# The last additions of a routed FFN, shared between VectorE and GpSimd

## What is computed

```python
def _L3_ffn_ref(x, gate_w, gate_b, w1, b1, w2, b2):
    flat = x.reshape(-1, D)
    logits = flat @ gate_w + gate_b
    topv, topi = lax.top_k(logits, TOP_K)                 # TOP_K = 2 of E = 8
    topw = jax.nn.softmax(topv.astype(jnp.float32), axis=-1)
    routing = jnp.zeros_like(logits).at[jnp.arange(T)[:, None], topi].set(topw)
    def body(acc, params):
        W1e, b1e, W2e, b2e, we = params
        h = jax.nn.gelu(flat @ W1e + b1e, approximate=False)
        return (acc + (h @ W2e + b2e) * we[:, None], None)
    final, _ = lax.scan(body, init, (w1, b1, w2, b2, routing.T))
...
x = x + jnp.tanh(g_ffn[3]) * _L3_ffn_ref(_layernorm(x, axis=-1), ...)
```

## Time and profile before

| | us |
|---|---|
| median of 3 runs | 1948.7 |
| the three runs | 1950.23, 1944.82, 1948.7 |
| span of the profiled execution | 1942.7 |
| busy in it: TensorE / VectorE / ScalarE / GpSimd | 1620.1 / 1242.5 / 1210.7 / 740.3 |

### The profile page before, as it was taken

How to read it: one execution, slowest core, us unless ns; L and a number is a source line. 1 busy time by engine, 2 the same in 40 slices (tenths; PEclk the granted TensorE clock), 3 DMA queues, 4 the chain that set the end, 5 groups by cost and what they waited for, 6 DMA issues and landing times. The chain is left out here.

```text
span 1942.7 us, 38924 instructions
## 1 busy us (share of the span) xinstructions
PE 1620.1 (83%) x12739; PEld 1206.0 (62%) x12739; DVE 1242.5 (64%) x3348; ACT 1210.7 (62%) x4192; POOL 740.3 (38%) x712
## 2 busy tenths in 40 slices
PE   4399999599999769999789966999579887866994
PEld 3355554379999546666589855545456555644994
DVE  5599999488888666767567755213457656654444
ACT  2189999189999557877667742433168656631444
POOL 2145555245555542111067835002222332333542
PEclk9799999699999889999889987999689888977997
DMA  3320000110000042423191022100044433313224
GB/s 127 74 106 1 1 1 1 34 45 2 1 2 2 28 116 76 105 72 89 32 320 54 1 88 86 42 0 1 19 121 114 124 101 84 88 55 97 70 70 156
DMA packets 63845, 126.40 MB, mean 65 GB/s; under 512 B 10670, under 2 KB 27233, under 8 KB 61529
## 3 DMA queue, kind: packets, MB, share of 16 engines
q1 hardware_dynamic: 53658, 103.10, 18.6%
q10 hardware_dynamic: 5616, 12.06, 1.9%
q0 software_dynamic: 4384, 8.89, 1.3%
HBM read 91.00 MB, written 50.43 MB: 73 GB/s over the span
## 5 line engine op out<-in xcount | busy, mean ns | idle before, releaser
L1531 ACT ACTIVATE L_E<-L_sc,L_negm 128x128 f32<-128x128 f32 x1024 | 300.1, 402 | 153.2 <-DVE L_negm L1399 152.5
L593 ACT ACTIVATE B_E<-B_logits,B_m 128x32 f32<-128x32 f32 (+1 forms) x1792 | 365.2, 374 | 8.8 <-DVE B_m L562 7.9
L599 POOL TENSOR_TENSOR B_E<-B_E,B_r 128x512 f32<-128x512 f32 x256 | 268.0, 1047 | 264.5 <-DVE B_r L581 264.5
L1399 DVE TENSOR_REDUCE L_negm<-L_sc 128x4 f32<-128x512 f32 x256 | 174.9, 686 | 87.0 <-PE L_sc L1640 74.9
L562 DVE TENSOR_REDUCE B_m<-B_logits 128x16 f32<-128x512 f32 (+1 forms) x256 | 172.8, 675 | 38.4 <-PE B_logits L553 31.2
L1638 PE MATMUL L_sc<-KS,L_QS 128*128 128x512 f32 x256 | 143.8, 562 | 54.5 <-DMA L_QS<-L_qsplit 37.1
L576 DVE TENSOR_REDUCE B_r<-B_E 128x16 f32<-128x512 f32 (+1 forms) x256 | 172.9, 675 | 2.5 <-POOL B_E L599 1.3
L1539 ACT ACTIVATE L_PT<-L_pt 128x512 f32<-128x512 f32 x256 | 165.9, 649 | 6.3 <-DMA picked_rows<-A_ys 6.0
L1648 PE MATMUL L_pt<-ident,L_E 128*128 128x128 f32 x1024 | 160.1, 280 | 0.8 <-ACT L_PT L1539 0.8
L551 PE MATMUL B_logits<-B_phihi,B_xhi 128*128 128x512 f32 x256 | 153.5, 600 | 5.1 <-DVE B_philo L538 2.5
L1648 PEld LDWEIGHTS L_pt<-ident,L_E 128*128 128x128 f32 x1024 | 126.6, 145 | 23.9 <-issue 2.5
(11 more groups left out here) (348 smaller groups left out, 3598.5 us busy)
## 6 DMA issues: line engine op xcount, KB each, us to landing
route_rows<-in_F_fill SPq DMA_DIRECT2D x33, 516.0 KB, 19.7
KS<-L_ksplit SPq DMA_DIRECT2D x180, 64.0 KB
L_QS<-L_qsplit SPq DMA_DIRECT2D x42, 256.0 KB
F_xg<-route_rows SPq DMA_DIRECT2D x71, 64.5 KB
ew<-in_expert_w SPq DMA_DIRECT2D x1, 4096.0 KB, 15.4
L_cT<-in_ctxT SPq DMA_DIRECT2D x16, 256.0 KB
L_qsplit<-L_qhi ACTq DMA_DIRECT2D x16, 256.0 KB, 2.7
L_qsplit<-L_qlo ACTq DMA_DIRECT2D x16, 256.0 KB, 5.8
```

The costliest lines, as they stand in the source:

```text
L593: ins = nc.scalar.activation(e[:, cols], self.bank(k)[:, cols], ACT.Exp, bias=self.m[:, k % 4, g:g + 1])
L599: self.st.nc.gpsimd.tensor_tensor(e, e, self.r[:, k % 2, :].unsqueeze(2) .to_broadcast([128, self.ng, self.size]), ALU.mult).then_inc(self ...
L1399: nc.vector.tensor_reduce(negm[:, k % 4, :], sc[k % 2][:].rearrange("p (h k) -> p h k", h=NHG), AX.X, ALU.max, negate=True).then_inc(s["ma ...
L1531: ins = nc.scalar.activation(e[:, h * 128:(h + 1) * 128], sc[k % 2][:, h * 128:(h + 1) * 128], ACT.Exp, bias=negm[:, k % 4, h:h + 1])
```

## The change

The adds of groups 1, 3, 5 and 7 go to GpSimd, behind its last scatter; VectorE keeps those of groups 0, 2, 4 and 6. The semaphore `x_new` becomes two, `x_new0` counted by VectorE and `x_new1` by GpSimd, and SP waits on them in turn.

```diff
@@ semaphores
-            "y_ps", "y_out", "init_ps", "init_used", "part_sum", "scaled", "x_new", "stored")}
+            "y_ps", "y_out", "init_ps", "init_used", "part_sum", "scaled", "x_new0", "x_new1", "stored")}
@@ sync
             for n in range(NG):
-                sp.wait_ge(s["x_new"], n + 1)
+                sp.wait_ge(s[f"x_new{n % 2}"], n // 2 + 1)
                 sp.dma_start(out[:, n * GB:(n + 1) * GB, :], xgroup(p, n)).then_inc(s["stored"], 16)
@@ gpsimd
             for i in range(NT):
                 bring(i)
+            for n in range(1, NG, 2):
+                g.wait_ge(s["part_sum"], n + 1)
+                g.wait_ge(s["scaled"], n + 1)
+                cols = slice(n * GB, (n + 1) * GB)
+                nc.gpsimd.tensor_tensor(xgroup(p, n), yl[0][:, cols, :], yl[1][:, cols, :], ALU.add).then_inc(s["x_new1"], 1)
@@ vector, total(n)
-                nc.vector.tensor_tensor(xgroup(p, n), yl[0][:, cols, :], yl[1][:, cols, :], ALU.add).then_inc(s["x_new"], 1)
+                nc.vector.tensor_tensor(xgroup(p, n), yl[0][:, cols, :], yl[1][:, cols, :], ALU.add).then_inc(s["x_new0"], 1)
@@ vector
                 ins.then_inc(s["part_sum"], 1)
-                if n:
+                if n % 2:
                     total(n - 1)
-            total(NG - 1)
```

## The result

| | before | with the change |
|---|---|---|
| median, 20 runs each (us) | 1944.73 | 1950.84 |
| lowest to highest | 1936.09 to 1951.29 | 1941.11 to 1960.34 |
| span of the profiled execution | 1942.7 | 1952.9 |

The ratio is 1.0034, with a 95% interval of 1.0020 to 1.0047: some 6 us slower, 4 to 9 by the interval. The forecast was +2.0. The time lies in the range, the sign was right, and two thirds of the loss were not foreseen. That the median of 1950.84 stands beside a forecast of 1950.7 is luck: the forecast added +2.0 to the median of three runs, 1948.7, and the median of twenty is 1944.73. The base was 4.0 us too high and the change priced 4.1 too low.

A forecast was written before the change was run, and what follows sets the result against it. VectorE was taken to bound the tail, with only its last 1 to 2 us to be bought. 3.24 + 1.13 - 2.40 = +1.97 us, on the median 1948.7, gave 1950.7 us; range 1945.5 to 1954.3.

The forecast's parts named there:

- four adds off VectorE: VectorE's tail loses four adds of 0.60 us each: 2.40 us off its chain.
- three adds of GpSimd in its stream: GpSimd's adds of groups 1, 3, 5 take turns with VectorE, costing it 1.08 us each: +3.24 us.
- the fourth, behind VectorE's last: GpSimd's add of group 7 ends 1.13 us after VectorE's last add: +1.13 us.
- last add: End of the tail's last add, on GpSimd: moves from 1938.99 to 1940.96, +1.97 us.
- last store, issue to landing: SP's store of group 7, issued in an idle queue, lands 2.1 us after issue, as before.
- closing: From the last store's landing to the kernel's end: 1.6 us, as before.
- The estimate from the Trainium skill: Exclusive turns held for whole instructions, 115 ns on each side: 4 x (1.27 + 2 x 0.115) - 2.40 = +3.6 us.
- The forecast signs: GpSimd adds 1.27 to 1.6 us, neighbouring VectorE instructions beyond 1 us, VectorE tail 13.0, last add's end at 14.2.
- Side by side: Rival 1: VectorE and GpSimd do not collide in the tail, -1.2 us, 1947.5; chance 0.15.
- Starvation of GpSimd: Rival 2: GpSimd's four adds come only when VectorE is through, +3.0 us, 1951.7; chance 0.22.
- rival 3: Each VectorE tail instruction loses its overlap and pays a gap as the port changes hands, +9.4 us, 1958.1; chance 0.04.
- rival 4: GpSimd's adds fall in VectorE's pauses, or the measured difference is that between runs: 1948.7; chance 0.09.

The follow-up runs named there:

- e4: Changed kernel without GpSimd's four adds, odd groups stored without their sum; no timed ratio, the end comes 14.7 us after group 1's first VectorE instruction.
- e1: Changed kernel with one more GpSimd DRAIN directly behind its last scatter, ahead of its four adds; timed 1.0017 (0.9993 to 1.0040).
- e3: Changed kernel, GpSimd drained behind its last scatter, VectorE's tail reading PSUM in place of a second SBUF tensor; no timed ratio, last add ends at 11.0 us.
- e6: Changed kernel, GpSimd drained behind its last scatter, X copied to eight PSUM banks by VectorE during its wait; timed 0.9987 (0.9969 to 1.0005) against before.
- e2: Kernel before, all adds on VectorE, plus a 128x4 GpSimd memset waiting for the last add; timed 1.0021 (0.9996 to 1.0046).
- e2b: Kernel before with the late GpSimd memset and a DRAIN directly behind the last scatter; no timed ratio, tail 16.0 us.
- e5: Changed kernel with one more GpSimd DRAIN ahead of the last eight scatters; single time 1954.45, tail 17.7 us.

## Why the prediction was right and wrong

By its own steps (tail's clock):

| step | forecast | measured |
|---|---|---|
| four adds off VectorE | -2.40 | -2.40 (e4: 12.25 to 9.85) |
| three adds of GpSimd in its stream | +3.24 (1.08 each) | +3.0 (1.0 each, e1 against e4) |
| the fourth, behind VectorE's last | +1.13 | +1.1 |
| last add | +1.97 | +1.74 |
| last store, issue to landing | 2.1, as before | 2.0 |
| closing | 1.6, as before | 6.6: **+5.0** |

*Right*: that the engines take turns, where the forecast put them and near its price. Rows 8 and 9 gave both halves of a turn, with the handover's overlap in them. The estimate from the Trainium skill's SBUF — State Buffer (the part above its section "Who interferes with whom"), with 0.115 us on each side and no overlap, was +3.6 us and the trace has +1.74, so the price by the rows was the better one. The rule of the Trainium skill itself (SBUF — State Buffer, section "Who interferes with whom": two SBUF inputs on VectorE contend with a GpSimd instruction that reads SBUF) held in the changed kernel, e3 and e6. The forecast signs showed, with one exception: adds of 1.44 to 1.65 us, a VectorE tail of 12.9 us (forecast 13.0), the last add's end at 13.99 (14.2), and VectorE instructions held to 1.35 us beside the adds of groups 3 and 5. Beside that of group 1 the longest is 0.72, because VectorE spent the other part of that turn waiting for its load.

*Wrong*: the sentence that GpSimd has nothing queued before or behind its adds, and "store and closing follow as before". Behind the adds stood GpSimd's DRAIN, with 87 scatters issued since the DRAIN before. It was in the trace of before as a DRAIN of 9.1 us ending at 1925.6, under the loads, and I had looked only at rows that count as busy, which ended at 1918.4. A look at what each engine's queue does between its last instruction and the barrier would have given the missing term from rows of before: the forecast has the last add end at 1940.96, the DRAIN 7.2 us later at 1948.2, and SP through at 1941.3 + 2.0 = 1943.3, so +4.9. With it the sum is +6.9, against +6.1 by the medians and +6.6 by the traces. On the base of the forecast that makes 1955.6, above the top of the range, 1954.3; on the median of twenty runs it makes 1951.6. The range had no term for the closing and held by its high base alone: the same range on 1944.73 would end at 1950.3, below the measured 1950.84.

*The rivals.* Side by side (-1.2) isn't what this kernel does, but its price was near for the kernels without turns: e3 -0.9, e6 -1.1, e4 -1.3. In all three the last store, issued earlier, took longer to land (2.5, 2.4 and 2.8 us against 2.1). Starvation of GpSimd fell: its adds stand at 1.4, 5.0, 8.6 and 12.4 us, one per two groups. A gap at each VectorE instruction (rival 3, +9.4) fell as well: they start 0.26 us apart in the tail, but for the ones held. It was the only rival with more than the +6 that was measured, and it named the wrong mechanism. "Nothing visible" (rival 4) falls by the interval of the twenty runs.

*What the timed runs bear out.* The +6 of the changed kernel stands clear of its interval. The division into 1.7 and 5.0 comes from traces, one execution of each kernel; the timed ratios of e1 and e2 agree with it and are each too wide to prove it alone. What the DRAIN does for each scatter isn't visible; only that the time goes by their number (8, 48, 78, 87) and not by what follows them.

## What to carry to other kernels

An engine whose list of work ends early may still be doing something in the shadow of the others: before it is given work at the end, look at its closing DRAIN, not only at its busy rows. Where GpSimd has issued DMAs of its own and something must follow them late, a DRAIN placed in its idle time pays the price before anybody waits (e1, e2b), but one in the midst of the scatters holds up the next of them (e5). And GpSimd's adds of two SBUF tensors ran beside VectorE unhindered here only where VectorE read one SBUF tensor (e3, e6); with two on each side an add moved off VectorE (0.60 us) costs it 1.0.

## What the runs showed of the hardware that was not expected

- GpSimd's DRAIN takes about 0.083 us for each indirect DMA issued since the DRAIN before (0.7 us after 8, 4.0 after 48, 6.5 after 78, 7.2 after 87), also long after they have landed (e2), and the same whether a scatter, an add or a memset is the last instruction. Where none was issued since, it ends within 0.1 us of the instruction ahead (e1, e2b).
- A wait at the barrier is put down to TensorE's queue in the rows of waits where GpSimd was the late one.
- VectorE's copies of X from SBUF to PSUM, 0.68 us per 128x512, ran between the last scatters without a visible price: the scatters beside them take 0.96 us, with the idle times of the other runs (0.94, 0.83, 0.30).
